# Graph layers on one core: when the first layer counts its dense edges, and when the count table is multiplied

## The reference, cut to what matters

```python
sender_features = nodes[senders]
msg_in = jnp.concatenate([sender_features, edges], axis=-1)
messages = msg_in @ W_message
agg = jax.ops.segment_sum(messages, receivers, num_segments=total_nodes)
h = _layer_norm(jax.nn.relu(agg) + nodes, ln_aggr_scale, ln_aggr_bias)
nodes_out = _relu_mlp_skip(h, [mlp_W0, mlp_W1, mlp_W2], [mlp_b0, mlp_b1, mlp_b2])
nodes_new = _layer_norm(nodes + nodes_out, ln_out_scale, ln_out_bias)
```

## Time and profile before

| | before |
|---|---|
| median of three runs | 1525.03 us (1520.14 to 1525.53) |
| profiled execution | 1522.61 us |
| its span | 1520.8 us |
| PE busy | 1140.0 us, 75% of the span |
| DVE busy | 824.7 us, 54% |
| POOL busy | 743.8 us, 49% |
| mean granted PE clock | 0.854 of full |
| gathers of the first layer (L751) | 260, from 39.6 to 376.5 us |

### The profile page before, as it was taken

The page is one execution under the profiler, slowest core; times in us unless marked ns, Lnnn a source line. Parts: engine busy times, 40 slices in busy tenths (PEclk is TensorE's granted clock), DMA queues, the critical chain, the costliest instruction groups (busy, mean ns, idle before and its releaser), DMA issues. The chain is left out here.

```text
span 1520.8 us, 29090 instructions
## 1 busy us (share of the span) xinstructions
PE 1140.0 (75%) x7379; PEld 987.7 (65%) x7380; DVE 824.7 (54%) x2697; ACT 436.1 (29%) x1412; POOL 743.8 (49%) x818
## 2 busy tenths in 40 slices
PE   1587989888997549999994667748888995699800
PEld 1477888787886438999993333327767784599700
DVE  7455778788666451111113899847775235644344
ACT  4201112122221123444443444340000001355433
POOL 5777777777000023222223655247667770444375
PEclk9979899999998569999997899965589885899955
DMA  5644454544112029999994222143334344144365
GB/s 183 173 128 127 125 139 136 133 133 134 49 46 53 7 82 345 348 351 349 353 337 163 70 83 83 48 157 107 102 94 119 117 122 132 60 123 127 114 177 154
DMA packets 191245, 223.62 MB, mean 147 GB/s; under 512 B 69906, under 2 KB 152996, under 8 KB 190874
## 3 DMA queue, kind: packets, MB, share of 16 engines
q1 hardware_dynamic: 156674, 132.93, 26.9%
q0 software_dynamic: 32064, 87.29, 20.2%
q10 hardware_dynamic: 2392, 2.06, 0.5%
HBM read 190.48 MB, written 32.04 MB: 146 GB/s over the span
## 5 line engine op out<-in xcount | busy, mean ns | idle before, releaser
L751 POOL DMA_INDIRECT O0G<-n_rows,src_tab x260 | 258.9, 996 | 90.0 <-issue 87.0
L751 POOL DMA_INDIRECT O1G<-sparse_rows,src_tab x188 | 180.8, 962 | 102.8 <-issue 89.3
L768 PE MATMUL O0ps_sums<-O0OH,O0G 128*128 128x80 f32 x1040 | 141.5, 294 | 41.7 <-DMA O0G<-n_rows,src_tab 35.7
L768 PEld LDWEIGHTS O0ps_sums<-O0OH,O0G 128*128 128x128 f32 x1040 | 134.5, 209 | 48.7 <-issue 34.9
L1836 POOL DMA_INDIRECT e0xs<-token_rows,e0idx x64 | 60.7, 948 | 195.0 <-ACT e0idx L1905 193.2
L1957 DVE TENSOR_TENSOR e0ys<-e0ps_y,NR 128x256 f32<-128x256 f32 x64 | 27.2, 425 | 221.7 <-PE e0ps_y L1876 221.7
L768 PEld LDWEIGHTS O1ps_sums<-O1OH,O1G 128*128 128x128 f32 x752 | 118.3, 244 | 18.9 <-issue 16.5
L768 PE MATMUL O1ps_sums<-O1OH,O1G 128*128 128x80 f32 x752 | 119.0, 327 | 14.4 <-DMA O1G<-sparse_rows,src_tab 7.8
L1862 PE MATMUL e0ps_h<-e0xT,e0W 128*128 128x128 f32 x1024 | 127.6, 279 | 2.3 <-DMA e0W<-in_L_ffn_w 2.3
L1862 PEld LDWEIGHTS e0ps_h<-e0xT,e0W 128*128 128x128 f32 x1024 | 122.2, 195 | 2.6 <-DMA e0W<-in_L_ffn_w 2.5
L1876 PE MATMUL e0ps_y<-e0W,e0hidT 128*128 128x256 f32 x512 | 121.1, 380 | 0.0
(11 more groups left out here) (371 smaller groups left out, 2497.7 us busy)
## 6 DMA issues: line engine op xcount, KB each, us to landing
e0W<-in_L_ffn_w SPq DMA_DIRECT2D x128, 512.0 KB, 5.8
O0EA<-in_edge_attr SPq DMA_DIRECT2D x97, 128.0 KB
expert_out<-e0ys SPq DMA_DIRECT2D x64, 128.0 KB, 5.2
expert_out<-e1ys SPq DMA_DIRECT2D x56, 128.0 KB, 1.9
O0G<-n_rows,src_tab POOLq DMA_INDIRECT x260
e1W_all<-in_L_ffn_w SPq DMA_DIRECT2D x16, 256.0 KB, 5.8
n_rows<-NR SPq DMA_DIRECT2D x5, 640.0 KB
token_rows<-O0N SPq DMA_DIRECT2D x25, 128.0 KB, 2.3
```

Source lines behind the costliest of these rows:

```text
L751: pool.indirect_dma_start(out=self.G[:, s, k, :], out_offset=None, in_=self.rows_dram, in_offset=bass.IndirectOffsetOnAxis(ap=src_tab[:, g ...
L768: last = nc.tensor.matmul(self.ps[o % 2][0:rows.shape[1], half * P:half * P + WINDOW], rows, self.OH[:, h, k, 0:WINDOW], start=(k == 0), s ...
```

## The change

It sets the three numbers that spread units and pieces over the steps. What is computed, the tables, the number of instructions and the groups and tiles of each step stay as they are.

```diff
-    UNIT_STEPS = next(u for u in range(STEPS0) if plan0.groups_before(u) >= NS)
-    FIRST_PASS_BY, PASSES_BY = plan0.step_of(T - DENSE_TILES), plan0.step_of(T - DENSE_TILES + 1) - 1
-    assert UNIT_STEPS < FIRST_PASS_BY < PASSES_BY <= STEPS0
+    GATHER_STEPS = next(u for u in range(STEPS0) if plan0.groups_before(u) >= NS)
+    UNIT_STEPS = GATHER_STEPS * 3 // 4
+    FIRST_PASS_BY, PASSES_BY = GATHER_STEPS + 1, GATHER_STEPS + 6
+    assert UNIT_STEPS < FIRST_PASS_BY <= plan0.step_of(T - DENSE_TILES) and FIRST_PASS_BY < PASSES_BY < plan0.step_of(T - DENSE_TILES + 1)
```

## The result

The changed kernel takes 1532.87 us (median of 12 runs, 1523.61 to 1542.6), the one before, run beside it, 1524.24 us (12 runs, 1520.14 to 1526.98). The ratio is 1.0055 with a 95% interval of 1.004 to 1.007: slower by 8.6 us, where 3.9 us faster was forecast, and outside the range that ended at 1530. The profiled execution took 1531.53 us, span 1529.8, clock 0.846.

The account below looks back on a forecast made before the run. Gathers were taken to bound the kernel up to step 19, with DVE a hidden second bound, then PE. Part 1, Part 2 and the lag of parts 3 and 4 gave −10.9 − 1 + 8 = −3.9 us: 1521 us, range 1511 to 1530.

Parts of the forecast that it names:

- part 3: Steps 0 to 6: eight earlier units hidden; 7 to 14: eight more, 14.4 us against DVE's 10.3 of waits, lag 6.
- Part 4: Steps 15 to 19: pieces come in, 17.3 us of PE, units leave; +3 us of lag, between 0 and 5.
- Part 1: Steps 20 to 24: eight 256-column pieces leave, six 128-column ones come; 66.5 us becomes 55.6, −10.9 us.
- Part 2: Steps 26 to 28: six 128-column pieces leave; −1 us, between −4 and 0.
- the clock: Steps 26 to 28: the half clock comes three steps sooner, +2 us each, +6 at most; 1528 us, chance 0.08.
- DVE becomes the bound and the gathers stop: Steps 7 to 14: units paid in full, none of DVE's waits filled, lag of 20 us; 1533 us, chance 0.07.
- gathers that end later than 380 us: End of the gathers, forecast near 377 us: ending after 380 us would show the DVE rival, chance 0.07.
- absorbed lag: End of step 19: units and pieces fill DVE's and PE's gaps, PE only 2 us late; 1515 us, chance 0.34.
- likeliest case: Whole layer: gain and lag as in the sum; 1521 us, own range 1516 to 1527, chance 0.51.

Follow-up runs that it names:

- e1: The changed kernel with its early units in steps 0 to 14, but pieces in steps 20 to 28 as before the change; 1.0041 against the kernel before.
- g1: The kernel before the change, run unchanged against itself; 1.0024.
- m1: m0 with the freed PSUM bank used for the odd units' products; 0.9953 against the kernel before, 1650.58 us.
- m0: The changed kernel with the third layer's and turned-back products sharing one PSUM bank, and two more PE waits; 1.0052 against the kernel before, 1667.11 us.

## Why the prediction was wrong

**The step that failed** is part 3, "DVE can take 10.3 of that out of its waits", and the lag of 6 us taken from it. It was 12.9 us, over the bound of 9 that the prediction set. The sum closes on DVE. Steps 7 to 14 took 136.9 us before, of which DVE waited 10.3; they take 148.8 now, of which it waits 6.4. Outside its waits it needs 142.4 − 126.6 = 15.8 us more, 1.97 per unit for eight units, the price of the earlier trace rows and not the 1.8 taken. DVE's "issue" waits before additions rose from 13 to 20, seven for the eight new units; 12 of the 35 units have neither this gap nor a wait for PE. Of the 10.3 us only 3.9 were filled: 15.8 − 3.9 = 11.9. The part's own sum left 4.1 us; the other 7.8 are 1.4 of price and 6.4 of waits that stayed. With all of its waits filled DVE would still have been 5.5 us late, so on this chip about half of the lag is work that had no room and half is waiting in turn. Another 1.0 us came along from steps 0 to 6, costed at nothing. The prediction had named the reason, PE and DVE waiting for each other in turn with two units in a last place, but gave it 5 us as a bound; PE's waits for additions grew by 17.9 us (4.0 to 21.9), and the granted clock of the stretch fell from 0.93 to 0.87.

**Part 4** was right in kind (PE full, DVE with room, full clock, no wait for gathers) and cost 0.6 us instead of 3. Parts 3 and 4 together: 13.5 instead of 8, 5.5 us off.

**Part 1** held: −10.2 for −10.9. Steps 20 and 21 took 25.4 us for 26.7, with the stall at the join (3.96 us against 3.85 in the earlier trace rows), steps 22 to 24 took 30.9 for 28.9.

**Part 2** was +0.2, not −1. Of its rival, the clock, little came: 0.93 from 456 to 482 us, then 0.52, where it had been 1.00 and 0.60. The Trainium skill (TensorE: Matmul & The Clock Gate, "Why this matters for your kernels") warns of idle gaps between bursts of matmuls; the trace agrees more plainly in step 13, where a gap of 3.95 us stood ahead of a group at 3.62 instead of 1.91 us, at a granted clock of 0.50.

**The rivals.** "DVE becomes the bound and the gathers stop" was given 0.07 and a lag of 20 us. Its place, its engine and the full price of a unit were right. Its time, 1533 us, is also the measured median, but that is luck: it needs a lag of 20 us and stopped gathers. PE's lag stayed at 13.5 us, and the gathers were held up by little (POOL's waits for slots went from 3.0 to 7.3 us). Its sign, gathers that end later than 380 us, came true only by the late start: 381.7 us, 378.8 net. On the slower chips they were held up in earnest, from 18.4 us of such waits in the kernel before to 50.9 in the changed one, and still the ratio was the same. The absorbed lag (0.34) was furthest off. Both it and the likeliest case read DVE's waits as room.

**What stays open.** The layer accounts for 3.5 us of the profile's difference, the errors of the four parts (5.5 + 0.7 + 1.2 = 7.4) for its distance from −3.9. The median says 8.6 us, so some 5 us are not located: late start, rest of the program, or executions unlike the profiled one (they spread over 19 us after, over 7 before). On the slower chips e1 points to the early units (1.0041, near what g1 shows for noise, and gone with 17 steps), and alternation at the one bank is shown by m1 against m0. On the first kind of chip both are read from the waits and the step starts of one execution each, and two banks were tried there only with 17 steps and with the old spread. So the cause of the measured 8.6 us is argued there, not shown.

## What to carry over

A wait of an engine is room for more work only if the work can start in it: here 3.9 of 10.3 us could be used. Where two engines hand one PSUM bank back and forth, price each further hand-over at its full time and expect waits on both sides; look at the fullest step and not only at the mean, and try a second bank before packing them closer. On the slower chips it turned a loss of 0.5% into a gain of 0.5%. Where moved work frees 10 us of a bound engine, look for what has to run earlier to make room, and price that at the full unit.

## What the hardware showed unexpectedly

After a gap of 3.95 us on PE the next 16 matmuls of 128 by 80 took 3.62 us, at a granted clock of 0.50, where 16 such matmuls took 1.91 at 1.00. Chips differ: the same kernel took 1524 us on some and 1657 to 1668 us on others (mean granted clock of the kernel before 0.854 against 0.819). On the second kind DVE's additions wait "remote" for products that the trace shows done, 39.6 us in 9 waits up to 450 us in the kernel before, up to 6.8 us at a time. DVE's waits up to 400 us hold no such row on the first chip, before or after. What DVE waits for in them was not found.
